# Attention in a two-layer decoder: K transposed without padding, two heads in 32 rows, and copied to SBUF twice

## The reference

```
q = proj(x, Wq, bq);  k = proj(ctx, Wk, bk);  v = proj(ctx, Wv, bv)      # 16 heads of 16
# layer 0 only: q and k are rotated (cos, sin)
attn_w = softmax(q @ k.T / 4)                                            # per head, 128 x 128
out = (attn_w @ v) @ Wo.T + bo
```

## Time and profile before

| what | value |
|---|---|
| runs | 1011.43, 1013.15, 1012.89 us; median 1012.89 |
| profiled execution, own time | 1011.7 us |
| its span in the profile | 1009.8 us |
| mean granted TensorE clock | 0.958 |
| PE busy | 901.5 us (89%) |
| DVE busy | 616.3 us (61%) |
| ACT busy | 509.3 us (50%) |
| POOL busy | 298.1 us (30%) |

### The profile page before, as it was taken

How to read it: one execution, slowest core, us unless ns; L and a number is a source line. 1 busy time by engine, 2 the same in 40 slices (tenths; PEclk the granted TensorE clock), 3 DMA queues, 4 the chain that set the end, 5 groups by cost and what they waited for, 6 DMA issues and landing times.

```text
span 1009.8 us, 20264 instructions
## 1 busy us (share of the span) xinstructions
PE 901.5 (89%) x7498; PEld 720.3 (71%) x7498; DVE 616.3 (61%) x1820; ACT 509.3 (50%) x1205; POOL 298.1 (30%) x480
## 2 busy tenths in 40 slices
PE   3569999999987989989999999989999999879990
PEld 2346777768766766667777878768788888779980
DVE  4999887675682798876854778667554444003203
ACT  1335646345547545465454665574635654336642
POOL 4323322212430253422221433324221133214424
PEclk9779999999999989999999999989999999999995
DMA  9999000000100000000000032211301257989954
GB/s 320 408 319 317 11 2 12 11 2 16 32 28 6 17 33 26 19 6 11 1 17 17 17 104 77 78 70 60 125 27 53 63 166 247 369 287 387 403 214 177
DMA packets 39425, 115.01 MB, mean 114 GB/s; under 512 B 5464, under 2 KB 21600, under 8 KB 38688
## 3 DMA queue, kind: packets, MB, share of 16 engines
q1 hardware_dynamic: 35584, 103.46, 29.4%
q0 software_dynamic: 3744, 10.26, 2.7%
HBM read 99.25 MB, written 37.70 MB: 136 GB/s over the span
## 4 chain that ended last, share of the span: by engine, by line
PE 72%; DVE 12%; ACT 6%; issue 5%; DMA 4%; POOL 1%; SPq 1%; ACTq 0%; DVEq 0%; POOLq 0%
PE ps L707 51%; PE ps L712 8%; PE ps L719 6%; PE ps L783 3%; DMA EW<-moe_w 2%; ACT PT L1427 2%; DVE PT L1111 2%; DMA work<-xs_d 1%; PE ps L850 1%; PE ps L1008 1%; ACT slot_rows L1427 1%; DVE stat L1047 1%; PE ps L884 1%; DVE PT L1098 1%; PE ps L893 1%
## 5 line engine op out<-in xcount | busy, mean ns | idle before, releaser
L1615 POOL TENSOR_TENSOR stat<-stat,mhalf 128x1 f32<-128x1 f32 x112 | 66.2, 592 | 337.6 <-DVE stat L1049 337.4
L707 PE MATMUL ps<-wall,slot_rows 128*128 128x256 f32 (+1 forms) x448 | 136.7, 431 | 10.5 <-ACT KB L1454 8.4
L707 PEld LDWEIGHTS ps<-wall,slot_rows 128*128 128x128 f32 x448 | 80.2, 197 | 33.5 <-issue 21.0
L1111 DVE TENSOR_REDUCE PT<-ps 128x8 f32<-128x1024 f32 x64 | 75.3, 1218 | 28.2 <-PE ps L719 28.2
L719 PE MATMUL ps<-KB 32*128 32x128 f32 (+1 forms) x2048 | 78.2, 290 | 10.5 <-ACT slot_rows L1427 3.9
L719 PEld LDWEIGHTS ps<-KB 32*128 32x128 f32 (+1 forms) x2048 | 66.0, 192 | 29.3 <-issue 25.8
L712 PE MATMUL ps<-cst,PT 128*128 128x128 f32 x512 | 76.0, 284 | 11.7 <-DVE PT L1111 4.1
L712 PEld LDWEIGHTS ps<-cst,PT 128*128 128x128 f32 x512 | 61.0, 146 | 28.1 <-issue 14.1
L707 PE MATMUL ps<-wgu,slot_rows 128*128 128x352 f32 x256 | 79.5, 462 | 1.5 <-ACT PT L1432 0.8
L707 PE MATMUL ps<-slot_rows,wall 128*128 128x128 f32 x640 | 78.4, 277 | 0.3 <-DVE slot_rows L1121 0.2
L707 PEld LDWEIGHTS ps<-slot_rows,wall 128*128 128x128 f32 x640 | 74.7, 192 | 4.9 <-issue 1.3
(11 more groups left out here) (228 smaller groups left out, 1859.6 us busy)
## 6 DMA issues: line engine op xcount, KB each, us to landing
EW<-moe_w SPq DMA_DIRECT2D x30, 514.0 KB, 4.2
EW<-moe_w SPq DMA_DIRECT2D x30, 512.0 KB
PT<-moe_w SPq DMA_DIRECT2D x12, 514.0 KB, 8.5
PT<-moe_w SPq DMA_DIRECT2D x12, 512.0 KB, 10.0
wall<-wts SPq DMA_DIRECT2D x1, 4104.0 KB, 20.2
work<-xs_d SPq DMA_DIRECT2D x31, 129.0 KB, 3.3
slot_rows<-ys_d SPq DMA_DIRECT2D x8, 384.0 KB, 7.1
KB<-ys_d SPq DMA_DIRECT2D x8, 384.0 KB, 5.9
```

The lines of the kernel that those rows point to most:

```text
L707: last = k.e.matmul(o, a, b, start=(i == 0), stop=(i == len(pairs) - 1))
L1111: e.tensor_reduce(peak[:, 2 * p:2 * p + 2, :, DH], s4, AX.X, ALU.max).then_inc(emptied[u.at], 1)
L1615: return k.e.tensor_tensor(v[:, 7:8], v[:, 8:9], mhalf[:, :], ALU.pow)
```

## The change

- K is written without padding (`rowsK` is 256 wide), so that it takes 2 transposes for 4. In each block of 32 rows now stand two heads, 16 rows each.
- ACT copies the two blocks of PSUM to SBUF twice: once with the second head's rows at zero and -1 in row 16, once with the first head's rows at zero and -1 in row 0. K's four quarters in SBUF are these.
- Q stays padded, in four quarters. Its features are put in another order on the host (`by_quarters` on Wq and bq), so that quarter `c` holds every second head. In odd quarters the window of 128 columns starts 16 columns earlier, so that a head's rows are the second half of its 32, and its maximum lies in row 0.
- The first scores now contract 32 rows as well. The maximum's row has to be zero there: POOL writes zeros over it (`peaks`, a memset before "with bo"), and PE waits for that ahead of Q's transposes (`"no peak"`).
- The planned durations follow: PE 0.9 to 0.7 for the transposes of K and Q, ACT 0.69 to 0.9 for K's copy, POOL 0.72 to 0.87.

```diff
-    yield piece(0.95, [Q], [("p", 0.72, (n, "bo", a)), ("D", 0.42, Q)], [("F", "bo", a)])
+    yield piece(0.95, [Q], [("p", 0.87, (n, "bo", a)), ("D", 0.42, Q)], [("F", "bo", a)])
...
-    yield piece(0.9, [kT, qT], [("A", 0.69, kT), ("A", 0.57, qT)], [V])
+    yield piece(0.7, [kT, qT], [("A", 0.9, kT), ("A", 0.57, qT)], [V])
...
         def rowsK(s):
-            return PT[s][:, 0:NC * P]
+            return PT[s][:, 0:D]
 
         def rowsQ(s):
-            return PT[s][:, NC * P:2 * NC * P]
+            v = PT[s][:, D:D + NC * QW].rearrange("p (c m w) -> p c m w", c=NC, w=HR)
+            return v[:, :, 0:NR, 0:DH]
+
+        def peaks(s):
+            v = PT[s][:, D + DH:D + DH + NC * QW].rearrange("p (c r) -> p c r", c=2)[:, :, 0:2 * P]
+            return v.rearrange("p c (e n w) -> p c e n w", e=2, w=HR)[:, :, :, :, 0]
+
+        def quarter(s, c):
+            at = D + c * QW - c % 2 * DH
+            return PT[s][:, at:at + P]
...
-            for name, made, src in (("kT", "kv", rowsK(s)), ("qT", "q", rowsQ(s))):
+            for name, made, src in (("kT", "kv", [rowsK(s)[:, c * P:(c + 1) * P] for c in range(2)]),
+                                    ("qT", "q", [quarter(s, c) for c in range(NC)])):
...
                 k.wait_ge(memsets, 4 + NS)
-                pe_transpose(k, u, src, NC)
+                if name == "qT":
+                    k.wait_ge(gpsimd[s], count(GPSIMD, n, "no peak", a))
+                pe_turn(k, u, src)
...
-            pe_scores(k, pair, QT(s), KT(s), DH)
+            pe_scores(k, pair, QT(s), KT(s))
...
-                e.tensor_reduce(peak[:, 2 * p:2 * p + 2, :, DH], s4, AX.X, ALU.max).then_inc(emptied[u.at], 1)
+                e.tensor_reduce(peak[:, 2 * p:2 * p + 2, :, :], s4, AX.X, ALU.max).then_inc(emptied[u.at], 1)
...
-            e.activation(KT(s), ps[:, u.at, :], ACT.Identity, scale=k_("kkeep"),
-                         bias=k_("kminus")).then_inc(emptied[u.at], 1)
+            for i in range(2):
+                ins = e.activation(KT(s).rearrange("p (c e k) -> p c e k", e=2, k=P)[:, :, i, :], v3(ps[:, u.at, 0:D], P),
+                                   ACT.Identity, scale=k_("kkeep")[:, i:i + 1], bias=k_("kminus")[:, i:i + 1])
+            ins.then_inc(emptied[u.at], 1)
...
             x = u_["xT", a]
             k.wait_ge(emptied[x.at], x.out)
+            k.wait_ge(memsets, 4 + NS)
+            e.memset(peaks(s), 0.0).then_inc(gpsimd[s], 1)
```

More of the change, by code:

```diff
@@ L42 @@
 PTW = H * P // 2 + HR
+QW = 160
 XW = D + 2
@@ L65 @@
 COLS = [("q", 2), ("k", 2), ("ld", 2), ("nw", 2), ("gamma", 2), ("beta", 2), ("b1", F1C), ("bv0", 2), ("bv2", 2)]
-CONST = [("cos", DH), ("sin", DH), ("ident", P), ("block", P), ("mask8", HC), ("dest", 2 * B), ("dump", 8), ("iota", E), ("kkeep", 1),
-         ("kminus", 1), ("before", P), ("region0", E), ("region1", E), ("tiles", NTMAX)]
+CONST = [("cos", DH), ("sin", DH), ("ident", P), ("block", P), ("mask8", HC), ("dest", 2 * B), ("dump", 8), ("iota", E), ("kkeep", 2),
+         ("kminus", 2), ("before", P), ("region0", E), ("region1", E), ("tiles", NTMAX)]
 def spans(table):
@@ L112 @@
 SCALAR = ["squared", "squared", "v", "abs", "silu", "silu", "abs", "abs", "gelu", "v"]
-GPSIMD = ["rs", "root", "with bo", "turned", "turned", "root", "xq", "hq", "hq", "root", "root", "root", "twice", "root",
-          "with bo", "root"]
+GPSIMD = ["rs", "root", "no peak", "with bo", "turned", "turned", "root", "xq", "hq", "hq", "root", "root", "root", "twice", "root",
+          "no peak", "with bo", "root"]
 def count(steps, n, name, i=0):
@@ L611, in decoder_kernel, with head_of @@
         vector_step = sem("vector_step")
+        def head_of(c, n):
+            return c // 2 * 2 * NR + 2 * n + c % 2
         def v3(ap, n):
@@ L713, in pe_transpose, with pe_turn, pe_scores @@
             last.then_inc(filled[u.at], 1)
-        def pe_scores(k, pair, lhsT, rhs, rows_):
+        def pe_turn(k, u, parts):
+            for c, part in enumerate(parts):
+                last = k.e.transpose(ps[:, u.at, c * P:(c + 1) * P], part, ident)
+            last.then_inc(filled[u.at], 1)
+        def pe_scores(k, pair, lhsT, rhs):
             for c in range(NC):
                 for n in range(NR):
-                    lane, at = slice(n * HR, n * HR + rows_), pair[n // 2].at + n % 2
+                    lane, at = slice(n * HR, (n + 1) * HR), pair[n // 2].at + n % 2
                     last = k.e.matmul(ps[:, at, c * P:(c + 1) * P], lhsT[lane, c * P:(c + 1) * P],
@@ L766, in pe_attention @@
                 k.wait_ge(emptied[x.at], x.out)
-            pe_transpose(k, u, rowsQ(s), NC)
+            pe_turn(k, u, [quarter(s, c) for c in range(NC)])
             yield
@@ L772, in pe_attention @@
             k.wait_ge(emptied[x.at], x.out)
-            pe_scores(k, pair, KT(s), QT(s), HR)
+            pe_scores(k, pair, KT(s), QT(s))
             yield
@@ L1084, in dve_attention @@
             k.wait_ge(scalar[s], count(SCALAR, n, "v", a))
-            dst = v3(AT[:, s, :], DH) if rope else padded(rowsK(s))[:, :, 0:DH]
-            e.tensor_tensor(dst, v3(ps[:, u.at, 0:D], DH), v3(bk, DH), ALU.add).then_inc(emptied[u.at], 1)
+            dst = AT[:, s, :] if rope else rowsK(s)
+            e.tensor_tensor(dst, ps[:, u.at, 0:D], bk, ALU.add).then_inc(emptied[u.at], 1)
             yield
@@ L1089, in dve_attention @@
             k.wait_ge(filled[u.at], u.full)
[L1090 to L1091 removed]
+            dst = quarters(Z[:, s, :]) if rope else rowsQ(s)
+            e.tensor_tensor(dst, quarters(ps[:, u.at, 0:D]), quarters(bq), ALU.add).then_inc(emptied[u.at], 1)
             yield
             if rope:
[L1094 to L1096 removed]
+                cosb = bc(k_("cos").unsqueeze(1).unsqueeze(1), NC, NR, DH)
+                for i, (src, dst, made) in enumerate(((AT, quarters(rowsK(s)), "kv"), (Z, rowsQ(s), "q"))):
+                    x = u_[made, a]
                     k.wait_ge(emptied[x.at], x.out)
[L1098 removed]
+                    cos_done = k.step(e.tensor_tensor(dst, quarters(src[:, s, :]), cosb, ALU.mult))
                     yield
@@ L1981, in image_t, with by_quarters @@
         return m.reshape(B, P, 2, P).transpose(0, 3, 2, 1).reshape(B * P, D)
+    def by_quarters(m):
+        return m.reshape(2, NR, 2, DH, -1).transpose(0, 2, 1, 3, 4).reshape(m.shape)
     cat = np.concatenate
-    w = {"oT": a["L0_attn_o_w"].T, "q0": a["L0_xattn_Wq"].T,
+    w = {"oT": a["L0_attn_o_w"].T, "q0": by_quarters(a["L0_xattn_Wq"]).T,
          "kv0": cat([a["L0_xattn_Wk"].T, a["L0_xattn_Wv"].T], 1), "o0": a["L0_xattn_Wo"].T,
@@ L2021 @@
              "tiles": np.tile(np.arange(NTMAX, dtype=np.float32), (P, 1)),
-             "kkeep": (np.arange(P) % HR < DH).astype(np.float32)[:, None],
-             "kminus": -(np.arange(P) % HR == DH).astype(np.float32)[:, None]}
+             "kkeep": np.stack([np.arange(P) % HR // DH == i for i in range(2)], 1).astype(np.float32),
+             "kminus": -np.stack([np.arange(P) % HR == i for i in (DH, 0)], 1).astype(np.float32)}
     arrays = {
```

27 lines of the change are left out of this document (11 added, 16 removed).

## The result

| | before | changed |
|---|---|---|
| median of runs beside each other | 1011.19 us (8 runs) | 1018.21 us (8 runs) |
| lowest to highest | 1006.34 to 1013.15 | 1016.99 to 1019.97 |
| profiled execution's span | 1009.8 us | 1014.9 us |
| PE busy | 901.5 us | 893.3 us |

The ratio is 1.0079, with a 95% interval of 1.0056 to 1.0102. Single executions of one kernel lie wide apart: those of the kernel before took from 1004.5 to 1017.7 us over all that were made for this document. So a time rests on medians, and a profiled execution is one of them. The forecast was 1006.5 us with a range to 1015. It is wrong in sign and outside its range, by 3 us at the upper end.

The account below looks back on a forecast made before the run. PE's work was taken to bound the kernel from 80 to 850 us. 1011.7 - 6.3 (transposes) + 0.5 (ACT's copies) = 1005.9 us, or 1007.1 by the median; forecast 1006.5 us, range 998 to 1015.

Parts of the forecast that it names:

- PE's transposes, -6.3 us: PE, K's transposes: 64 fewer, 60 of them where PE is the time; -6.3 us, between 0 and -7.0.
- The price by spacing (0.109 us): PE, K and Q transposes: eight overlapping ones take 0.87 us, so each removed one is worth 0.109 us.
- the one by whole length (18 us): Rival on PE: each removed transpose saves its whole 0.284 us, 18.2 us in all, giving 994.0 us; chance 0.02.
- Scores, maxima, memset, each 0: PE's 32-row scores, DVE's maxima with another stride, POOL's added memset: 0 each; upper ends 1.3, 4.4 and 3.3 us.
- ACT's two copies, +0.5 us: ACT, K's copy: the pair takes 1.02 us for 0.78; +0.5 us on the time, between 0 and +7.7.
- become the bound: Rival on ACT: all 7.7 us of K's extra copying lie on the path, giving 1013.7 us; chance 0.03.
- Two tiles leave the slow stretch: Rival at batch 0's last tiles: two moved ahead of the last router matmul gain 4.7 us, giving 1001.8 us; chance 0.15.
- The router holds batch 1: Rival at batch 1's start: the last router matmul comes only 1.7 us earlier, 5.3 us lost, giving 1011.8 us; chance 0.11.
- Two places have a price: New order of all engines: only batch 0's moved tiles and ACT's table loads were priced, each taken as 0.
- The slower rival: ACT table loads between exponentials and silu or gelu make PE idle: 1013.4 to 1020.3 us; chance 0.14.
- PE's idle time between 80 and 850 us grows by more than 3 us: Sign in the changed profile, in the stretch PE bounds, that would show the prediction wrong.
- Batch 1's first transposes: Sign in PE's timeline at batch 1's start: at about 889 us for 896 before.

Follow-up runs that it names:

- the old order: Changed kernel with the three planned durations put back, so all five engines keep the order of before: 1005.84 us, ratio 0.9969 to the kernel before.
- the new one: Kernel before with only the change's three planned durations, so old operations in the changed kernel's order: 1023.92 us, ratio 1.0139 to the kernel before.
- the nine orders of these same operations: Changed operations under nine sets of planned durations, the changed kernel's and the old ones among them: ratios 0.9939 to 1.0100 to the kernel before.
- Without the loads: Changed operations with tanh for silu and gelu, leaving one table load: 996.18 us in the changed kernel's order, 983.88 us in that of before.
- the two made here: Changed operations, old three planned durations, DVE's planned `avT` duration 0.72 moved to 0.71 or 0.75: 1019.41 us (ratio 1.0097) and 1007.25 us (0.9954).

## Why the prediction was wrong, point by point

- **PE's transposes, -6.3 us: right in size, perhaps a little high.** With the +0.5 us of ACT the forecast for the operations was 5.8 us. In the old order they save 4.2 us by the medians and 3.1 us by the ratio (1.1 to 5.2), in the new one 5.7 us (1023.92 - 1018.21). PE's busy time fell by 8.2 us in the changed kernel, but over the nine orders of these same operations it is 887.3 to 896.5 us, which is 5.0 to 14.2 us less than before, so it doesn't price the transposes closely. The price by spacing (0.109 us) held, and the one by whole length (18 us) did not: nothing near it was saved in either order.
- **Scores, maxima, memset, each 0: nothing speaks against it.** All have their old lengths or the predicted ones, and together they left the gain in place in the old order; no run prices one alone. In the scores, 32 records of about 290 ns take 1.17 us, nearly eight at a time, where the prediction took four. PE waited once for the memset, for 0.8 us, in the changed kernel, where "no wait of PE that ends on POOL" was expected, and never in the old order.
- **ACT's two copies, +0.5 us: right in the pair's length.** The pair takes 1.02 us. PE's waits that end on K's copy, between 80 and 850 us, are 2.6 us in the old order for 1.7 us before. With the same order the whole change gained, so the copies did not become the bound.
- **"Two tiles leave the slow stretch": they took their work with them and nothing else.** The prediction reckoned with 2 x 6.1 us out of the stretch and, net, 4.7 us gained. The stretch is 6.2 us shorter, against 5.3 us of work put ahead of the router: 0.9 us net. PE's idle time in the stretch stayed (48.70 - 38.21 = 10.5 us, and 42.47 - 31.82 = 10.7 us), so each tile left there took 42.47 / 6 = 7.1 us for 6.1.
- **"The router holds batch 1": nearly equal ends, as written, for another reason.** The prediction set 5.3 us against 4.7 and took 0. The measured pair is 5.3 against 6.2 us, so its 0 for this place came out, though neither the gain of 4.7 us nor a hold by the router's routing was what happened. The miss is not in this place.
- **The step that failed: "Two places have a price", and for both "I take 0".** The order was new on all engines, and I priced the two places that I could name. All that is "the same work a place earlier or later" had no term at all. The cost came from there: 13.3 us between 80 us and the last router matmul. From 80 us to batch 1's start the changed kernel takes 12.4 us more than the same operations in the old order: PE is idle for 10.1 us more (45.8 + 10.7 us for 35.8 + 10.5 us) and busy for 2.3 us more. The additional waits end mostly on maxima that stand behind other samples' work on DVE (11.7 us for 4.8, 5.4 us of it at once); those that end on exponentials grew by 1.0 us only. The busy time goes with a granted clock of 0.98 for 0.99, as behind the 5.4 us wait, where it was 0.50.
- **The slower rival: right time by luck, wrong mechanism.** It put the loss on a bubble of table loads. Without the loads the orders still differ by 12.3 us, and where the old order has its bubble the new one is better, not equal (3.8 us idle for 8.5). It should have been "any order may be worse by 1%", with a chance of its own that doesn't rest on a pattern found in it. The whole chance of a slower kernel, 0.14, hung on that pattern.
- **The signs that I had named worked.** "PE's idle time between 80 and 850 us grows by more than 3 us" is what the windows show: 12.3 us. Batch 1's first transposes, forecast for about 889 us, stand at 900.83 us in the changed kernel. In the old order they stand at 888.47 us, but in an execution that was the fastest of twelve.

What stays open: which single dependence makes the new order worse. The windows and waits give the sum and its largest piece, the maxima. No run took out the 5.4 us wait alone, and I haven't shown that the rest would not close up or open elsewhere if it went. The other orders that lose do it elsewhere in part: in the one with only ACT's number new, waits for maxima are 4.5 us, and those for ACT are 34.2 us for 23.7 in the old order.

## What to carry to other kernels

Where a planner writes the order of every engine, a change has two effects: its operations and its new order. Hold the order (new operations, old planned numbers) to measure the first, and shift numbers that mean nothing, so that the order departs early and late, to see how wide the second scatters. One such shift is not enough: of the two made here one cost 13.6 us and the other nothing. If the scatter is wider than the saving, as here, a prediction needs it as a case with a chance of its own. The gain should then be taken by choosing among several orders after the change: here the change's own planned durations gave one of the worse ones.
